# Counting graph edges by keys of destination and a third of the sources instead of by destination alone

## The chip, the cores and the metric

One core of a Trainium2 chip runs the whole kernel. The metric is device time of one execution in microseconds (us), lower is better. Three executions of the kernel before took 1249.06, 1245.67 and 1246.85 us, so the median is 1246.85 us.

## The reference, cut to what matters

The reference is a graph block over N = 1250 nodes with D = 1024 features and E = 20000 edges: a layer norm, a graph attention, a linear attention with Fourier features and an MLP, then a ternary feed-forward. Only the graph attention matters here:

```python
dst = jnp.minimum((1250 * uniform(20000) ** 2.0).astype(int32), 9999)
src, dst = src[argsort(dst)], dst[argsort(dst)]
e = jnp.exp(-leaky_relu(al[src] + ar[dst], 0.1))
rowsum  = segment_sum(e, src, N)
h_prime = segment_sum(e[:, None] * h[dst], src, N) / (rowsum[:, None] + 1e-5)
```

A weight depends only on the pair (src, dst). So the kernel first counts how often each pair occurs, a 1250 by 1250 matrix of small integers, and later multiplies a dense matrix of exponentials by the counts. The edges come sorted by destination, and low destinations are more frequent: the first 125 destinations have 6390 of the 20000 edges, the last 125 have 1048.

## The kernel before, in words

**Data.** The edges are cut into CHUNKS = 160 chunks of T = 125, one edge on each partition. `ends` holds source and destination of each edge as floats. Chunks are handled in groups of HOT = 3.

**A step.** For one chunk and one tile of destinations, VectorE (DVE) writes two matrices of zeros and ones: `hot_s` (125 edges by 1250 sources, line 418) and `hot_d` (125 edges by 125 destinations, line 420). TensorE (PE) multiplies them, as three matmuls of 418, 416 and 416 columns (THIRDS, line 487), and adds up in `p_cnt`, three PSUM banks for a tile, two tiles in turn. HOT slots of the one-hots let VectorE be three steps ahead: it waits on `s_used` (line 416), which line 488 raises, and TensorE waits on `s_hot`.

**The loops.** `tile_onehots(t)` and `count_tile(t)` run for the NT = 10 tiles of destinations. The chunks that touch a tile are known on the chip only, so both engines load the first and last chunk from `span_i` into registers (line 224) and run a hardware loop over groups of three chunks (lines 413 and 482). A chunk that touches two tiles is done in both, and the last group of a tile is filled up, so 60 groups or 180 steps are run (18, 8, 6, 5, 5, 4, 4, 4, 3 and 3 groups). Each tile begins and ends on TensorE with three matmuls of zeros (lines 480, 491).

**Interleaved with it**, by the table AFTER, are ten row tiles of a second layer norm. ScalarE (ACT) takes ten pairs of row sums first (`first_stats`), then scales rows (`normalise`, line 324). TensorE transposes tile i after count tile t if i is in AFTER[t] (line 470, eight transposes). ScalarE applies gain and shift to the eight pieces (`affine`, line 335) and writes the rounded part `x2_hi` (line 340). VectorE subtracts it (`keep_lo(i)`, line 406), which stands in VectorE's program before `tile_onehots(t+2)`. ScalarE also copies each counted tile out of PSUM as 16-bit integers (`keep_counts`, line 319, three instructions), and SyncE (SP) stores it to DRAM in two transfers (`core.move`, lines 82 and 83), from two slots in turn.

**Order at the end of this stage.** All engines meet at a barrier (line 153); then TensorE starts the projections (line 1571), and from there on it is nearly always busy. Much later `attend_over_edges` reads the counts back, a tile of sources at a time (`load_counts`, and one load at the end of the attention stage), for lines 1557 and 709 on VectorE.

Of the kernel before, what the change touches and what calls it, by code (L numbers as in the profile page):

```python
# [6 lines left out]
ALU = mybir.AluOpType  # L7
# [20 lines left out]
HOT = 3  # L28
FF = 512
# [118 lines left out]
def count_and_second_norm(core):  # L148
# [4 lines left out]
    with ExitStack() as ctx:  # L153
# [11 lines left out]
        iota_h = over_lo.put("iota_h", [T, N], FP16)  # L165
        iota_t = over_lo.put("iota_t", [T, NT, 128], FP16)
        tab = over_lo.put("tab", [NT, 3, CHUNKS], F32)
        hit = over_lo.put("hit", [NT, 3, CHUNKS], F32)
        row2 = over_lo.put("row2", [NT, 2, CHUNKS], F32)
        span = over_keys.put("span", [NT, 4], F32)  # L170
        span_i = over_keys.put("span_i", [1, 2, NT], I32)
        hot_s = over_lo.put("hot_s", [T, HOT, N], BF16)
        hot_d = over_keys.put("hot_d", [T, HOT, 128], BF16)
        zeros = over_keys.put("zeros", [T, T], BF16)
        zero_rows = over_keys.put("zero_rows", [T, 418], BF16)
# [6 lines left out]
        p_cnt = ps("p_cnt", [128, 2, 3, 512])  # L182
# [11 lines left out]
        s_iotat = core.sem("tile_iotas_ready")  # L194
# [9 lines left out]
        s_tile = core.sem("tile_counted")  # L204
# [14 lines left out]
        def kept(t):  # L219
            return core.x_in[:, t % 2, 0:N // 2].bitcast(U16)  # L220
# [8 lines left out]
        AFTER = {0: (), 1: (0,), 2: (1, 2), 3: (3, 4), 4: (5,), 5: (6,), 6: (7,), 7: (8,), 8: (9,), 9: ()}  # L229
# [4 lines left out]
        def _(sp):  # L234
# [9 lines left out]
            for t in range(NT):  # L244
                sp.wait_ge(s_kept, t + 1)
                core.move(sp, core.counts_dram[:, :, t, :].rearrange("i p s -> p i s"), kept(t).rearrange("p (i s) -> p i s", i=NT),
                          s_cst[t % 2])

        @block.gpsimd
        def _(pool):  # L250
            pool.memset(core.ident[:], 0.0).then_inc(s_prep, 1)
            pool.iota(iota_h[:], pattern=[[1, N]], base=0, channel_multiplier=0,
                      allow_small_or_imprecise_dtypes=True).then_inc(s_iota, 1)
# [3 lines left out]
            pool.memset(ends[:, CHUNKS:, :], -1.0).then_inc(s_pad, 1)  # L257
            pool.iota(tab[:, 0, :], pattern=[[0, CHUNKS]], base=0, channel_multiplier=T,
                      allow_small_or_imprecise_dtypes=True).then_inc(s_iota, 1)
            pool.iota(tab[:, 1, :], pattern=[[0, CHUNKS]], base=T, channel_multiplier=T,  # L260
                      allow_small_or_imprecise_dtypes=True).then_inc(s_iota, 1)
            pool.iota(tab[:, 2, :], pattern=[[1, CHUNKS]], base=-CHUNKS, channel_multiplier=0,
                      allow_small_or_imprecise_dtypes=True).then_inc(s_iota, 1)
# [38 lines left out]
        def _(act):  # L302
# [11 lines left out]
            def keep_counts(t):  # L314
                act.wait_ge(s_tile, t + 1)
                if t >= 2:
                    act.wait_ge(s_cst[t % 2], MOVED * (t // 2))
                for n, (a, w) in enumerate(THIRDS):
                    last = act.activation(kept(t)[:, a:a + w], p_cnt[0:T, t % 2, n, 0:w], ACT.Copy)
                last.then_inc(s_kept, 1)  # L320
# [23 lines left out]
            keep_counts(0)  # L344
            act.wait_ge(s_rstd, RSTD_STEPS)
            for i in range(NT):
                normalise(i)
                if i == 3:
                    keep_counts(1)
            act.wait_ge(s_gb, 1)  # L350
            for t in range(2, NT):
                for i in AFTER[t - 1]:
                    affine(i)
                keep_counts(t)
                if t == NT - 2:
# [5 lines left out]
        def _(dve):  # L361
# [3 lines left out]
            dve.tensor_reduce(bounds[:, 0, :], edges_f[:, 1], AX.X, ALU.min).then_inc(s_efl, 1)  # L365
            dve.tensor_reduce(bounds[:, 1, :], edges_f[:, 1], AX.X, ALU.max).then_inc(s_efl, 1)
            dve.wait_ge(s_iota, 1)
            dve.tensor_copy(iota_t[:, :, 0:T], iota_h[:].rearrange("p (a b) -> p a b", a=NT)).then_inc(s_iotat, 1)
            dve.wait_ge(s_tr, 1)
            dve.tensor_copy(row2[:].rearrange("p a (g c) -> p a g c", c=2),  # L370
                            p_bound[0:NT, 0:4 * EDGE_ROWS].rearrange("p (a c g) -> p a g c", a=2, c=2)).then_inc(s_ends, 1)
# [6 lines left out]
            dve.wait_ge(s_iota, 4)  # L378
# [20 lines left out]
            dve.tensor_copy(span_i[:], p_span[0:1, 0:2 * NT].rearrange("p (a t) -> p a t", a=2)).then_inc(s_span, 1)  # L399
            dve.wait_ge(s_span, 1)  # L400
            dve.wait_ge(s_iotat, 1)
# [6 lines left out]
            with dve.register("chunks_done") as done, dve.register("first_chunk") as r0, dve.register("past_chunk") as r1:  # L408
                dve.reg_mov(done, 0)

                def tile_onehots(t):
                    first, past = groups_of(dve, t, (r0, r1))
                    with dve.Fori(first, past, HOT) as g:
                        before = dve.snap(done, min_val=0, max_val=NT * (CHUNKS + HOT))
# [9 lines left out]
                tile_onehots(0)  # L424
                dve.wait_ge(s_vt, 1)
                dve.tensor_copy(core.cols[:], p_cols[:, 0:COLUMN_COUNT]).then_inc(s_gb, 1)
                tile_onehots(1)
# [4 lines left out]
                for i in AFTER[NT - 2]:  # L432
                    keep_lo(i)
# [5 lines left out]
        def _(pe):  # L439
# [3 lines left out]
            for a in range(2):  # L443
                for c in range(2):
                    pe.matmul(p_bound[0:NT, (2 * a + c) * EDGE_ROWS:(2 * a + c + 1) * EDGE_ROWS],
                              bounds[:, a, c:c + 1].to_broadcast([EDGE_ROWS, NT]), ident[0:EDGE_ROWS, 0:EDGE_ROWS],
                              start=True, stop=True)
# [2285 lines left out]
```

## Time and profile before

| | |
|---|---|
| median of three executions | 1246.85 us |
| the profiled execution, its own time | 1247.46 us |
| its span, from the first to the last instruction | 1245.7 us |
| TensorE busy | 1187.0 us |
| VectorE busy | 757.5 us |
| ScalarE busy | 704.7 us |
| GpSimd busy | 337.1 us |
| mean granted TensorE clock | 0.984 of full |

Times in the rows are microseconds from the span's start, busy times are sums. A queue's name with a q behind it (DVEq, SPq) is the engine's sequencer, which does register work, branches and waits and hands the other instructions to the engine.

### The profile page before, as it was taken

The page shows a single profiled execution, that of the slowest core. Times are in us where ns is not written, and L with a number is a line of the kernel's source. Part 1 is how long each engine was busy: PE and PEld are TensorE (multiplying, and loading weights), DVE is VectorE, ACT ScalarE, POOL GpSimd, SP SyncE. Part 2 cuts the span into 40 slices and gives each one's busy share as a digit, 9 for nine tenths or more (in the row PEclk, how much of TensorE's full clock was granted, in tenths as well). Part 3 has the DMA queues.
Part 4 walks back from the last instruction along what each step waited for, and adds up shares of the span by engine and source line. Part 5 has one row for each costly group of instructions (what it writes and reads, how often), then busy time and mean ns, then how long its engine had stood idle before and what let it go on. Part 6 is the DMA issues. An engine that isn't in the chain of part 4 may idle for free. (4 is left out here: it accounts for less than half of the span.)

```text
span 1245.7 us, 19482 instructions
## 1 busy us (share of the span) xinstructions
PE 1187.0 (95%) x6857; PEld 1040.2 (84%) x6857; DVE 757.5 (61%) x1248; ACT 704.7 (57%) x1070; POOL 337.1 (27%) x296
## 2 busy tenths in 40 slices
PE   6999998999999999999989999999989998999997
PEld 3555598999999999999978878999978877887884
DVE  7988815656665655665774676777753122556656
ACT  7265617777777777777786333322344332455543
POOL 1500013242414143333122010566635331211100
PEclk9999999999999999999999999999987999999999
DMA  8011140020201202020446566222253332712103
GB/s 221 11 21 29 32 96 1 1 71 0 71 21 50 63 8 71 0 71 0 138 126 215 165 194 203 77 87 87 76 184 99 99 80 71 218 33 66 30 6 99
DMA packets 72195, 99.41 MB, mean 80 GB/s; under 512 B 27242, under 2 KB 52166, under 8 KB 71632
## 3 DMA queue, kind: packets, MB, share of 16 engines
q1 hardware_dynamic: 68684, 86.11, 24.2%
q0 software_dynamic: 3456, 12.58, 3.4%
q8 instruction: 34, 0.56, 0.2%
q14 instruction: 21, 0.16, 0.0%
HBM read 77.04 MB, written 21.63 MB: 79 GB/s over the span
## 5 line engine op out<-in xcount | busy, mean ns | idle before, releaser
L1067 POOL TENSOR_TENSOR cos_sin_lo<-cos_sin,cos_sin_hi 125x1024 fp32r<-125x1024 f32 (+1 forms) x40 | 95.7, 2392 | 245.7 <-ACT cos_sin_hi L1179 245.7
L487 PE MATMUL p_cnt<-hot_s,hot_d 125*125 125x418 bf16 x540 | 113.7, 361 | 1.8 <-DVE hot_d L420 1.8
L418 DVE TENSOR_SCALAR hot_s<-iota_h,ends 125x1250 bf16<-125x1250 f16 x180 | 98.0, 544 | 14.5 <-PE p_cnt L487 12.5
L487 PEld LDWEIGHTS p_cnt<-hot_s,hot_d 125*125 125x125 bf16 x540 | 63.3, 139 | 51.5 <-DVE hot_d L420 40.5
L1571 PE MATMUL rows_in_psum<-x,mix_hi_v 128*128 128x416 f32 (+1 forms) x384 | 105.4, 356 | 0.0
L1571 PE MATMUL rows_in_psum<-x,mix_hi_q 128*128 128x416 f32 (+1 forms) x384 | 104.1, 352 | 0.0
L1571 PE MATMUL rows_in_psum<-x,mix_hi_k 128*128 128x416 f32 (+1 forms) x384 | 103.9, 351 | 0.0
L769 PE MATMUL rows_in_psum<-h_hi,a_lo 125*125 125x342 f32 x300 | 97.0, 323 | 5.9 <-POOL a_lo L611 3.8
L1675 PE MATMUL rows_in_psum<-x,xt_hi 128*125 128x512 f32 x320 | 100.4, 395 | 0.0
L769 PE MATMUL rows_in_psum<-h_hi,a_hi 125*125 125x342 f32 x300 | 96.4, 321 | 0.0
L769 PE MATMUL rows_in_psum<-h_lo,a_hi 125*125 125x342 f32 x300 | 96.4, 321 | 0.0
L1179 ACT ACTIVATE cos_sin_hi<-cos_sin 125x1024 fp32r<-125x1024 f32 (+1 forms) x80 | 83.6, 1045 | 8.2 <-PE rows_in_psum L1653 6.2
L1403 DVE TENSOR_SCALAR whole_turns<-rows_in_psum 125x512 f32<-125x512 f32 (+1 forms) x80 | 54.5, 681 | 39.3 <-PE rows_in_psum L1623 36.5
L2012 PE MATMUL rows_in_psum<-wo_rest,at_hi 128*125 128x512 f32 x280 | 77.4, 399 | 0.0
L1164 ACT ACTIVATE cos_sin<-part_turn 125x512 f32<-125x512 f32 (+1 forms) x80 | 49.8, 623 | 44.2 <-DVE part_turn L1405 43.8
L1571 PEld LDWEIGHTS rows_in_psum<-x,mix_hi_v 128*128 128x128 f32 x384 | 73.1, 191 | 1.0
L1571 PEld LDWEIGHTS rows_in_psum<-x,mix_hi_q 128*128 128x128 f32 x384 | 72.1, 188 | 0.7
L1571 PEld LDWEIGHTS rows_in_psum<-x,mix_hi_k 128*128 128x128 f32 x384 | 72.2, 188 | 0.5
L1571 PE MATMUL rows_in_psum<-x,mix_lo_v 128*128 128x416 f32 (+1 forms) x192 | 69.1, 360 | 3.7 <-PEq L153 3.5
L1675 PEld LDWEIGHTS rows_in_psum<-x,xt_hi 128*125 128x125 f32 x320 | 59.4, 186 | 13.7
L1675 PE MATMUL rows_in_psum<-x,xt_lo 128*125 128x512 f32 x160 | 65.4, 409 | 5.6 <-DVE x L1413 5.5
L1409 DVE TENSOR_TENSOR cos_sin_lo<-cos_sin,cos_sin_hi 128x1000 fp32r<-128x1000 f32 (+1 forms) x40 | 63.2, 1579 | 8.5 <-ACT cos_sin_hi L1179 8.0
(310 smaller groups left out, 3091.3 us busy)
## 6 DMA issues: line engine op xcount, KB each, us to landing
x_in<-in_x_dram SPq DMA_DIRECT2D x30, 448.0 KB
attn_dram<-attn_t SPq DMA_DIRECT2D x8, 625.0 KB, 4.0
at_in<-attn_dram SPq DMA_DIRECT2D x10, 500.0 KB, 4.7
x_rows<-in_x_dram SPq DMA_DIRECT2D x10, 448.0 KB
x_in<-gnn_dram SPq DMA_DIRECT2D x10, 448.0 KB
out_dram<-rows SPq DMA_DIRECT2D x10, 448.0 KB
mix_in_v<-in_L_mix_wv_dram SPq DMA_DIRECT2D x8, 512.0 KB, 6.0
mix_in_k<-in_L_mix_wk_dram SPq DMA_DIRECT2D x8, 512.0 KB, 4.7
```

The lines of the kernel that those rows point to most:

```text
L418: dve.tensor_scalar(hot_s[:, j, :], iota_h[:], ends[:, at, 0:1].rearrange("p a b -> p (a b)"), None, ALU.is_equal)
L487: last = pe.matmul(p_cnt[0:T, t % 2, n, 0:w], hot_d[:, j, 0:T], hot_s[:, j, a:a + w], start=False, stop=False)
L769: last = pe.matmul(p_o[0:T, i % 2, n, 0:H_COLS], stationary(left, i, d), right[:, d, cols], start=(d == 0 and m == 0), stop=(d == NT - 1 a ...
L1067: pool.tensor_tensor(full(cs_lo, k), full(cs, k), f32(full(cs_hi, k)), ALU.subtract).then_inc(s_cslo[0], 1)
L1164: act.activation(step_view(cs, k, 1), rows(part, k), ACT.Sin, scale=TWO_PI)
L1179: act.activation(full(cs_hi, k), full(cs, k), ACT.Copy).then_inc(s_cshi, 1)
L1403: dve.tensor_scalar(flat(whole, k), flat(p_p, k), MAGIC, -MAGIC, ALU.add, ALU.add).then_inc(s_whole, 1)
L1409: dve.tensor_tensor(full(cs_lo, k), full(cs, k), f32(full(cs_hi, k)), ALU.subtract).then_inc(s_cslo[1], 1)
L1571: last = pe.matmul(p_w[:, n, 0:w], left[which][:, k, :], right[:, k, a:a + w], start=(k == 0 and m == 0), stop=(k == K8 - 1 and m == 2))
L1675: last = pe.matmul(p_h(i)[:, n, :], left[i % 2][:, k, :], right[:, k, n * 512:(n + 1) * 512], start=(k == 0 and m == 0), stop=(k == K8 - 1 ...
L2012: last = pe.matmul(p_o[i % 2][0:T, n, :], left[i % 2][:, k, :], right[:, n * 512:(n + 1) * 512], start=(k == 0 and m == 0), stop=(k == K8 ...
```

## The change

The 1250 sources are cut in PARTS_OF_S = 3 parts of S_PART = 417. A key is 3 x destination + part, and there are 3750 keys. The tiles become WINDOWS = 30 windows of 125 keys, and the source one-hots are 420 columns wide instead of 1250. A window's counts are 125 keys by 417 sources, one PSUM bank, four windows in turn (TURNS). Before the tables are made, VectorE splits the edges into keys and sources within a part (five new instructions on 80 by 250 elements). AFTER is spread over the windows, ScalarE copies the first five windows before it normalises, and later normalises tile i+2 just before `affine(i)`.

By the reference's edges the 30 windows take 10, 5, 4, 3, 3, 3, 3 groups, then 22 windows of 2 and the last of 1: 76 groups or 228 steps, against 60 and 180.

```diff
+PARTS_OF_S = 3
+S_PART = -(-N // PARTS_OF_S)
+S_WIDTH = 420
+WINDOWS = NT * PARTS_OF_S
+KEY_SHIFT = N * PARTS_OF_S // 2
+BANK_PIECES = [(0, 420)]
+TURNS = 4 // len(BANK_PIECES)
...
-        iota_h = over_lo.put("iota_h", [T, N], FP16)
-        iota_t = over_lo.put("iota_t", [T, NT, 128], FP16)
+        iota_s = over_lo.put("iota_s", [T, S_WIDTH], FP16)
+        iota_k = over_lo.put("iota_k", [T, WINDOWS, 128], FP16)
...
-        p_cnt = ps("p_cnt", [128, 2, 3, 512])
+        p_cnt = ps("p_cnt", [128, TURNS, len(BANK_PIECES), 512])
...
-        AFTER = {0: (), 1: (0,), 2: (1, 2), 3: (3, 4), 4: (5,), 5: (6,), 6: (7,), 7: (8,), 8: (9,), 9: ()}
+        AFTER = {w: tuple(i for i in range(NT) if w == 6 + i + i // 2) for w in range(WINDOWS)}
+        FIRST_WINDOWS = 5
...
-            for t in range(NT):
+            for t in range(WINDOWS):
                 sp.wait_ge(s_kept, t + 1)
-                core.move(sp, core.counts_dram[:, :, t, :].rearrange("i p s -> p i s"), kept(t).rearrange("p (i s) -> p i s", i=NT),
-                          s_cst[t % 2])
+                core.move(sp, core.counts_of_keys[t * T:(t + 1) * T, :], kept(t), s_cst[t % 2])
...
+            pool.iota(iota_k[:, :, 0:T], pattern=[[T, WINDOWS], [1, T]], base=-KEY_SHIFT, channel_multiplier=0,
                       allow_small_or_imprecise_dtypes=True).then_inc(s_iota, 1)
...
-            keep_counts(0)
+            for t in range(FIRST_WINDOWS):
+                keep_counts(t)
             act.wait_ge(s_rstd, RSTD_STEPS)
-            for i in range(NT):
+            for i in range(2):
                 normalise(i)
-                if i == 3:
-                    keep_counts(1)
             act.wait_ge(s_gb, 1)
-            for t in range(2, NT):
+            for t in range(FIRST_WINDOWS, WINDOWS):
                 for i in AFTER[t - 1]:
+                    if i + 2 < NT:
+                        normalise(i + 2)
                     affine(i)
                 keep_counts(t)
...
+            split_step(dve.tensor_scalar(part_of_s[:], sources, float(S_PART), float(-KEY_SHIFT), ALU.is_ge, ALU.add))
+            for n in range(2, PARTS_OF_S):
+                split_step(dve.scalar_tensor_tensor(part_of_s[:], sources, float(n * S_PART), part_of_s[:], ALU.is_ge, ALU.add))
+            split_step(dve.scalar_tensor_tensor(keys, keys, float(PARTS_OF_S), part_of_s[:], ALU.mult, ALU.add))
+            dve.tensor_reduce(bounds[:, 0, :], keys, AX.X, ALU.min).then_inc(s_efl, 1)
+            dve.tensor_reduce(bounds[:, 1, :], keys, AX.X, ALU.max).then_inc(s_efl, 1)
+            split_step(dve.scalar_tensor_tensor(sources, part_of_s[:], float(-S_PART), sources, ALU.mult, ALU.add))
+            split_step(dve.tensor_scalar(sources, sources, float(-S_PART * KEY_SHIFT), None, ALU.add))
...
-                            dve.tensor_scalar(hot_s[:, j, :], iota_h[:], ends[:, at, 0:1].rearrange("p a b -> p (a b)"), None,
+                            dve.tensor_scalar(hot_s[:, j, :], iota_s[:], ends[:, at, 0:1].rearrange("p a b -> p (a b)"), None,
                                               ALU.is_equal)
-                            dve.tensor_scalar(hot_d[:, j, 0:T], iota_t[:, t, 0:T], ends[:, at, 1:2].rearrange("p a b -> p (a b)"),
+                            dve.tensor_scalar(hot_k[:, j, 0:T], iota_k[:, t, 0:T], ends[:, at, 1:2].rearrange("p a b -> p (a b)"),
                                               None, ALU.is_equal).then_inc(s_hot, 1)
...
-                for t in range(2, NT):
+                window_onehots(1)
+                for t in range(2, WINDOWS):
                     for i in AFTER[t - 2]:
                         keep_lo(i)
-                    tile_onehots(t)
+                    window_onehots(t)
...
-                            for n, (a, w) in enumerate(THIRDS):
-                                last = pe.matmul(p_cnt[0:T, t % 2, n, 0:w], hot_d[:, j, 0:T], hot_s[:, j, a:a + w], start=False, stop=False)
+                            for n, (a, w) in enumerate(BANK_PIECES):
+                                last = pe.matmul(p_cnt[0:T, t % TURNS, n, 0:w], hot_k[:, j, 0:T], hot_s[:, j, a:a + w], start=False, stop=False)
...
-                core.move(sp, counts[:, i % SLOTS], core.counts_dram[i], s_cnt[i % SLOTS])
+                core.move(sp, counts[:, i % SLOTS], core.counts_of_sources[:, :, i * T:(i + 1) * T], s_cnt[i % SLOTS])
...
-        core.counts_dram = nc.dram_tensor("counts_dram", (NT, T, NT, T), U16).ap()
+        core.counts_dram = nc.dram_tensor("counts_dram", (N, PARTS_OF_S * S_PART), U16).ap()
+        core.counts_of_keys = core.counts_dram.rearrange("d (a s) -> (d a) s", a=PARTS_OF_S)
+        core.counts_of_sources = core.counts_dram.rearrange("(t p) s -> p t s", p=T)
```

## Rows read from the trace of the kernel before

**Rows 1.** The page, part 1: busy time of each engine over the span.
```profile
PE 1187.0 (95%) x6857; PEld 1040.2 (84%) x6857; DVE 757.5 (61%) x1248; ACT 704.7 (57%) x1070; POOL 337.1 (27%) x296
```
**Rows 2.** Waits from 13 to 157 us: engine, tile, line, releaser, total, times, longest.
```profile
PEld p_cnt L487 <- DVE hot_d L420: 40.5, 152, 1.4
```
**Rows 3.** Timeline of VectorE: start, duration, engine, line, operation. One step of a tile.
```profile
118.10 0.55 DVE L418 TENSOR_SCALAR hot_s<-iota_h,ends 125x1250 bf16<-125x1250 f16 x1
118.56 0.26 DVE L420 TENSOR_SCALAR hot_d<-iota_t,ends 125x125 bf16<-125x125 f16 x1
118.72 0.54 DVE L418 TENSOR_SCALAR hot_s<-iota_h,ends 125x1250 bf16<-125x1250 f16 x1
```
**Rows 4.** VectorE's sequencer, line 413: all of them, then 119.3 to 121.1 us.
```profile
L413 DVEq FUSED_REGOPS  x60: 58/58/66, 12.9 to 149.7; - x60
...
L413 DVEq FUSED_REGOPS  x2: 58/58/58, 119.6 to 121.0; - x2
```
**Rows 5.** The same line from 65 to 65.9 us, between two tiles.
```profile
L413 DVEq COMPARE_BRANCH  x1: 50/50/50, 65.1 to 65.1; - x1
L413 DVEq FUSED_REGOPS  x1: 58/58/58, 65.8 to 65.8; - x1
```
**Rows 6.** VectorE's sequencer, line 413, at 49 to 50.4 us; PE's timeline before it.
```profile
48.56 0.69 PE L491 MATMUL p_cnt<-zero_rows,zeros 125*125 125x418 bf16 x3
...
L413 DVEq FUSED_REGOPS  x1: 58/58/58, 50.2 to 50.2; - x1
```
**Rows 7.** A `keep_lo` on VectorE's timeline, and line 413 behind it.
```profile
79.00 1.20 DVE L406 TENSOR_TENSOR x<-x_rows,x 128x1000 fp32r<-128x1000 f32 x1 [0.56 <-ACT x L340]
...
L413 DVEq FUSED_REGOPS  x1: 58/58/58, 79.7 to 79.7; - x1
```
**Rows 8.** Timeline of ScalarE, with the PE instruction that releases its copies.
```profile
51.85 4.64 ACT L324 ACTIVATE x_rows<-x_rows,ln_shift,ln_scale 125x1024 f32<-125x1024 f32 x4 [1.22 <-POOL ln_shift L299]
...
93.97 0.69 PE L491 MATMUL p_cnt<-zero_rows,zeros 125*125 125x418 bf16 x3
...
94.70 1.34 ACT L319 ACTIVATE x_in<-p_cnt 125x418 uint16<-125x418 f32 x3 [5.88 <-PE p_cnt L491]
95.91 2.90 ACT L335 ACTIVATE x_rows<-p_t,columns 128x125 f32<-128x125 f32 x8
98.84 1.04 ACT L340 ACTIVATE x<-x_rows 128x1000 fp32r<-128x1000 f32 x1
99.78 2.86 ACT L335 ACTIVATE x_rows<-p_t,columns 128x125 f32<-128x125 f32 x8
```
**Rows 9.** Line 487 at 13.5 to 17.4 us, then 20 to 40 us: minimum, median, maximum ns.
```profile
L487 PE MATMUL p_cnt<-hot_s,hot_d x10: 548/554/608, 13.9 to 17.1; 125*125 125x416 bf16 x6, 125*125 125x418 bf16 x4
...
L487 PE MATMUL p_cnt<-hot_s,hot_d x99: 339/341/391, 19.8 to 39.9; 125*125 125x416 bf16 x66, 125*125 125x418 bf16 x33
```
**Rows 10.** Timeline of the start: VectorE and GpSimd instructions like the added ones.
```profile
1.00 1.18 POOL L252 IOTA iota_h<- 125x1250 f16 x1
...
3.98 0.41 DVE L365 TENSOR_REDUCE bounds<-edges_f 80x2 f32<-80x250 f32 x1
...
10.05 0.23 DVE L393 TENSOR_SCALAR hit<-tab 10x160 f32<-10x160 f32 x1
```
**Rows 11.** Timeline of the stage's end, all engines.
```profile
152.62 0.69 PE L491 MATMUL p_cnt<-zero_rows,zeros 125*125 125x418 bf16 x3
...
154.06 1.31 ACT L319 ACTIVATE x_in<-p_cnt 125x418 uint16<-125x418 f32 x3
...
155.74 0.57 SPq L83 DMA_DIRECT2D counts_dram<-x_in  x1
...
156.84 0.43 PE L1571 MATMUL rows_in_psum<-x,mix_lo_v 128*128 128x418 f32 x1 [3.53 <-PEq L153]
```
**Rows 12.** The first load of the counts and the first instruction that reads it.
```profile
752.87 0.32 SPq L82 DMA_DIRECT2D counts<-counts_dram  x1
...
758.98 0.81 DVE L1557 SCALAR_TENSOR_TENSOR z<-z,counts 125x625 f32<-125x625 f32 x1 [0.80 <-ACT z L1352]
```

More of the change, by code:

```diff
@@ L164, in count_and_second_norm @@
         ends = over_keys.put("ends", [T, CHUNKS + HOT - 1, 2], F32)
-        iota_h = over_lo.put("iota_h", [T, N], FP16)
-        iota_t = over_lo.put("iota_t", [T, NT, 128], FP16)
[L167 to L173, printed above, removed]
+        part_of_s = over_lo.put("part_of_s", [EDGE_ROWS, 2, T], F32)
+        iota_s = over_lo.put("iota_s", [T, S_WIDTH], FP16)
+        iota_k = over_lo.put("iota_k", [T, WINDOWS, 128], FP16)
+        tab = over_lo.put("tab", [WINDOWS, 3, CHUNKS], F32)
+        hit = over_lo.put("hit", [WINDOWS, 3, CHUNKS], F32)
+        row2 = over_lo.put("row2", [WINDOWS, 2, CHUNKS], F32)
+        span = over_keys.put("span", [WINDOWS, 4], F32)
+        span_i = over_keys.put("span_i", [1, 2, WINDOWS], I32)
+        hot_s = over_lo.put("hot_s", [T, HOT, S_WIDTH], BF16)
+        hot_k = over_keys.put("hot_k", [T, HOT, 128], BF16)
         zeros = over_keys.put("zeros", [T, T], BF16)
-        zero_rows = over_keys.put("zero_rows", [T, 418], BF16)
+        zero_rows = over_keys.put("zero_rows", [T, 420], BF16)
         junk = over_lo.put("junk", [T, D], BF16)
@@ L256, in _ @@
                                base=0, pattern=[[-1, 128]], channel_multiplier=1).then_inc(s_ident, 1)
-            pool.memset(ends[:, CHUNKS:, :], -1.0).then_inc(s_pad, 1)
-            pool.iota(tab[:, 0, :], pattern=[[0, CHUNKS]], base=0, channel_multiplier=T,
+            pool.memset(ends[:, CHUNKS:, :], FLT_MAX).then_inc(s_pad, 1)
+            pool.iota(tab[:, 0, :], pattern=[[0, CHUNKS]], base=-KEY_SHIFT, channel_multiplier=T,
                       allow_small_or_imprecise_dtypes=True).then_inc(s_iota, 1)
-            pool.iota(tab[:, 1, :], pattern=[[0, CHUNKS]], base=T, channel_multiplier=T,
+            pool.iota(tab[:, 1, :], pattern=[[0, CHUNKS]], base=T - KEY_SHIFT, channel_multiplier=T,
                       allow_small_or_imprecise_dtypes=True).then_inc(s_iota, 1)
             pool.iota(tab[:, 2, :], pattern=[[1, CHUNKS]], base=-CHUNKS, channel_multiplier=0,
+                      allow_small_or_imprecise_dtypes=True).then_inc(s_iota, 1)
+            pool.iota(iota_s[:], pattern=[[1, S_WIDTH]], base=0, channel_multiplier=0,
+                      allow_small_or_imprecise_dtypes=True).then_inc(s_iota, 1)
+            pool.iota(iota_k[:, :, 0:T], pattern=[[T, WINDOWS], [1, T]], base=-KEY_SHIFT, channel_multiplier=0,
                       allow_small_or_imprecise_dtypes=True).then_inc(s_iota, 1)
@@ L444, in _ @@
                 for c in range(2):
-                    pe.matmul(p_bound[0:NT, (2 * a + c) * EDGE_ROWS:(2 * a + c + 1) * EDGE_ROWS],
-                              bounds[:, a, c:c + 1].to_broadcast([EDGE_ROWS, NT]), ident[0:EDGE_ROWS, 0:EDGE_ROWS],
+                    pe.matmul(p_bound[0:WINDOWS, (2 * a + c) * EDGE_ROWS:(2 * a + c + 1) * EDGE_ROWS],
+                              bounds[:, a, c:c + 1].to_broadcast([EDGE_ROWS, WINDOWS]), ident[0:EDGE_ROWS, 0:EDGE_ROWS],
                               start=True, stop=True)
+            pe.wait_ge(s_split, PARTS_OF_S + 2)
             for a in range(2):
@@ L455, in _ @@
             for a in range(2):
-                last = pe.transpose(p_span[0:1, a * NT:(a + 1) * NT], span[:, a:a + 1], ident[0:NT, 0:NT])
+                last = pe.transpose(p_span[0:1, a * WINDOWS:(a + 1) * WINDOWS], span[:, a:a + 1], ident[0:WINDOWS, 0:WINDOWS])
             last.then_inc(s_spant, 1)
@@ L474, in _, with count_window @@
                 pe.reg_mov(done, 0)
-                def count_tile(t):
-                    if t >= 2:
-                        pe.wait_ge(s_kept, t - 1)
-                    for n, (a, w) in enumerate(THIRDS):
-                        pe.matmul(p_cnt[0:T, t % 2, n, 0:w], zeros[:], zero_rows[:, 0:w], start=True, stop=False)
+                def count_window(t):
+                    if t >= TURNS:
+                        pe.wait_ge(s_kept, t - TURNS + 1)
+                    for n, (a, w) in enumerate(BANK_PIECES):
+                        pe.matmul(p_cnt[0:T, t % TURNS, n, 0:w], zeros[:], zero_rows[:, 0:w], start=True, stop=False)
@@ L488, in count_tile @@
                             last.then_inc(s_used, 1)
                         pe.reg_add(done, done, HOT)
-                    for n, (a, w) in enumerate(THIRDS):
-                        last = pe.matmul(p_cnt[0:T, t % 2, n, 0:w], zeros[:], zero_rows[:, 0:w], start=False, stop=True)
+                    for n, (a, w) in enumerate(BANK_PIECES):
+                        last = pe.matmul(p_cnt[0:T, t % TURNS, n, 0:w], zeros[:], zero_rows[:, 0:w], start=False, stop=True)
                     last.then_inc(s_tile, 1)
-                count_tile(0)
+                count_window(0)
@@ L495, in _ @@
                 pe.wait_ge(core.vectors_loaded, 16 * len(COLUMNS))
                 pe.transpose(p_cols[:, 0:COLUMN_COUNT], core.vectors[:], ident[0:COLUMN_COUNT, 0:COLUMN_COUNT]).then_inc(s_vt, 1)
-                for t in range(1, NT):
-                    count_tile(t)
+                for t in range(1, WINDOWS):
+                    count_window(t)
                     for i in AFTER.get(t, ()):
@@ L1050, in _ @@
                     sp.wait_ge(s_tern, 2 * PIECES)
-                    core.move(sp, core.counts[:, 0], core.counts_dram[0], s_cnt0)
+                    core.move(sp, core.counts[:, 0], core.counts_of_sources[:, :, 0:T], s_cnt0)
                 for n in TERNARY_AT.get(i - 4, ()):
```

46 lines of the change are left out of this document (22 added, 24 removed).

## The prediction

> **What bounds the kernel now.** I read the page's busy times first: TensorE is busy for 1187.0 of the 1245.7 us [rows 1]. Behind the counting stage it hardly ever waits, so what that stage gains or loses moves all the rest by as much. The question is when the first projection matmul starts; it does at 156.84 us [rows 11].
>
> Inside the stage the waits are next: TensorE's weight loads waited 152 times, 40.5 us in all, for the destination one-hot [rows 2]. So in steady counting VectorE is the bound. A step there goes from one `hot_s` to the next, 118.10 to 118.72, that is 0.62 us [rows 3]: 0.46 us for 1250 columns and 0.16 us for 125. Three steps are a group, 1.86 us, and 60 groups are 111.6 us of about 140.
>
> The last view is the one that decides here, VectorE's sequencer. Its loop on line 413 has register work, waits and a branch for every group. Where the engine behind it was busy with a `keep_lo` and the slots were free, the sequencer ran by itself, and went from one pass to the next in 121.0 - 119.6 = 1.40 us [rows 4]. That is hidden under 1.86 us now. It will not be hidden under a shorter group.
>
> **The change, part by part**, in times of the profiled execution, whose own time is 1247.46 us.
>
> *Width of the one-hots.* From 125 to 1250 columns a start-to-start distance grows by 0.30 us [rows 3], so 420 columns take 0.16 + 295 x 0.30 / 1125 = 0.24 us. A step of work is 0.24 + 0.16 = 0.40 us, a group 1.19 us (before rounding). The bounds for 420 columns are the two rows, 0.16 and 0.46 us. The sequencer's 1.40 us a group is longer than 1.19, so I take 1.40 us: 0.47 instead of 0.62 us a step, a quarter less and not the third that the width suggests.
>
> *Number of groups.* They grow from 60 to 76, as each window is rounded up to three chunks and shares chunks with its neighbours. 76 x 1.40 = 106.4 us against 60 x 1.86 = 111.6 us: only 5 us less.
>
> *Borders between windows.* From the last branch of a loop to the next loop it is 65.8 - 65.1 = 0.7 us [rows 5]; the branch stands 1.2 us into its pass, so a border adds (1.2 + 0.7 - 1.4), with the decimals that the rows round off some 0.6 us. The bounds are 0.5 and 0.7. Before, 10 borders were mostly hidden by queued work or `keep_lo`; now there are 30.
>
> *TensorE.* A step falls from three matmuls to one of 420 columns, and a window begins and ends with one matmul of zeros for three. It had slack already, so this frees no time by itself. From the start of the last group's pass to a counted window I reckon 2.06 us: third step after 0.95, one-hots 0.24 + 0.25 [rows 3], then 0.05 to the load, 0.39 for a matmul that has waited (the maximum in [rows 9]), 0.18 for the zeros. The slots suffice: one is free again 1.1 us after its `hot_s` began, under the 1.40 us of a group.
>
> *ScalarE and `keep_lo`, the chain.* Take window a, followed on TensorE by transposes of tile i; a+1, by those of i+1; and a+2, by none. That is the pattern from 6 to 20. When a is counted, ScalarE copies it (0.03 + 0.40, a third of 94.70 to 95.91, [rows 8]), normalises i+2 (1.13, a quarter of 4.64 with overlap), does eight pieces and the rounding of tile i (95.91 to 99.78 = 3.87), copies a+1 (0.40), normalises (1.13), and again 2.93 + 1.04 until `x2_hi` of i+1 is there [rows 8]. Sum 10.9 us. Only then can VectorE do `keep_lo(i+1)`, which stands ahead of window a+3; the next loop pass starts 0.7 us later [rows 7], and window a+3 is counted after 2 x 1.40 + 0.66. That is 15.1 us for three windows, against 3 x (2.8 + 0.6) + 0.2 = 10.4 us of VectorE's own and 11.2 us of ScalarE's. Both stand still part of the time. Before, tiles of three to six groups stood between `affine` and `keep_lo`, and hid more of this.
>
> *The start.* Three of the five new instructions stand ahead of the bounds. 250 columns took 0.41 us in a reduction, 160 took 0.23 us in a one-source instruction [rows 10]; with a wait behind each, 1.35 us. The two others lie beside TensorE's bounds matmuls. The key iota has 3750 columns for the 1250 that took 1.18 us [rows 10], some 3.5 us on GpSimd, ready by 7 us and needed at 14: nothing.
>
> *The sum.* First loop pass 12.9 [rows 4] + 1.35 = 14.3. Window 0, ten groups: 14.0, and 0.66 + 0.95 until the next loop (between those windows `columns` is copied; 49.25 to 50.2 [rows 6]): 29.9. Windows 1 to 6, 21 groups and six borders: 29.4 + 3.5, so 62.8, and window 6 is counted at 62.9. Five times 15.1, less 1.13 twice as tiles 8 and 9 have nothing more to normalise, 73.2: window 21 at 136.1. Windows 22 to 29, 15 groups and seven borders, 25.1, and 0.66: the last is counted at 161.8, where the last tile was at 153.3 [rows 11]. The end gets shorter: before, tile 9's `affine` and three copies lay between that and the barrier, 3.5 us to 156.84; now one copy (0.5), the issue of two stores (0.9) and the barrier (0.5), with `mix_lo` beside them: 2.0. The projections start at 163.8, **7.0 us later**.
>
> Two allowances. Loop passes are not everywhere that short (in one tile of ten the branch came back later), over the 56 groups on the path 1.2 us. And TensorE may run on its lower clock. At the start its matmuls took 554 ns and then 341 ns [rows 9], so a matmul is 0.21 us dearer at 1.2 than at 2.4 GHz; a link of the chain has one counting matmul and one of zeros, and there are seven links: 2.9 us if it stays low throughout, and I take half, 1.5.
>
> The clock is not sure, since a window that is warm uses TensorE for 0.18 of each 0.47 us. The Trainium skill, page "TensorE: Matmul & The Clock Gate", section "Part 1: The HAM clock gate", says that the half clock is the default and that activity releases it. By it the sum would be the whole 2.9 us instead of half if the new loop counts as too little activity, and none if it does not; no row of before shows a loop this sparse.
>
> *What costs nothing.* Stores: 30 pairs of transfers for 10, on a queue that mostly waited; a pair takes some 0.9 us to issue (0.32 in [rows 12] and 0.57 in [rows 11] for one transfer) and a window 3.4 us. They move 834 bytes a row instead of ten pieces of 250. The loads later have the small pieces instead, 1250 a tile. The one with least cover is issued at 752.87 and read at 758.98, after a wait for ScalarE and not for it [rows 12]: 6 us of cover, for a load of the piece size that stores had. If the cover is gone, a few us at most.
>
> Total 7.0 + 1.2 + 1.5 = 9.7 us: 1257.2 for the profiled execution. That lies 0.6 above the median, so **1256.6 us** for the median.
>
> **The rivals.** What this kernel's measurement can tell from no change is about 0.3%, 3.7 us, so the border of slower is 1250.6 and of faster 1243.1.
>
> *B, faster: ScalarE never stands still.* If `keep_lo` of tile i+1 does not hold up window a+3 until TensorE has run dry, the three windows take ScalarE's 11.2 us and not 15.1. Five times 3.9 less is 19.5: 1237.1. It decides as soon as three windows take under 12.4 us. For it: four PSUM banks in turn. Against it: VectorE does things in order, and waited for ScalarE ahead of `keep_lo` already [rows 7]. Chance 0.12.
>
> *C, no change: the sequencer does not bind.* If it keeps ahead of a 0.40 us step, 56 groups are 0.21 us cheaper, 11.8 us in all: 1244.8. Against it stand the passes of 1.40 us [rows 4], with nothing but the sequencer's own work in them. Chance 0.12; for a mixture with B, which also ends within 0.3%, 0.04.
>
> *D, slower by more: the clock stays low,* 2.9 instead of 1.5, and TensorE's transposes also hold up the slots at borders, a further 0.2 us at ten windows or more: 1260. For it, the sparse use; against it, that TensorE was at its full clock through most of the stage. Chance 0.18. A late load of counts or a slower `hot_s` (0.46 us at the upper bound, which would give today's 0.62 us step for 228 steps) would be slower still; 0.04.
>
> **How the numbers follow.** The forecast has 0.50; its own range is 1251.5 to 1260. With D and the late load, slower has 0.68 of the 0.72, as a corner of the forecast's own spread reaches below 1250.6. Faster is B, 0.12, and 0.03 of C's spread below 1243.1. Same has the rest, 0.17. The range from 1243 to 1262 leaves out B and the far end of D.
>
> **What would show it.** In the profile after: `hot_s` at 0.33 us busy and starts 0.47 us apart, in threes, inside a window; idle time of VectorE ahead of line `hot_s` put down to nothing or to "issue"; VectorE's `keep_lo` waiting for ScalarE's `x2_hi` some 2 to 5 us for most of ten tiles; windows 9, 12, 15 and 18 counted 15 us apart; the first projection matmul at 164 to 167 us; and behind it the same distance to the end as now. Starts 0.40 us apart would be C, windows three apart in 11 us B. The forecast is wrong if the projections start before 160 us, or if the time behind their start changes by over 2 us.

## The result, and the profile after

The changed kernel takes **1264.32 us** (median of 4 runs, 1260.66 to 1266.05), the kernel before, run beside it, 1246.53 us: a ratio of 1.0135, interval 1.0106 to 1.0165. It is slower, as forecast, but by 17.8 us where 9.7 were named, and beyond the end of the range. The profiled execution took 1266.05 us, its span is 1264.1 us.

The same view as [rows 1], part 1 of the page of the changed kernel:

```profile
PE 1177.9 (93%) x6545; PEld 1019.7 (81%) x6545; DVE 750.7 (59%) x1348; ACT 706.4 (56%) x1070; POOL 334.1 (26%) x297
```

TensorE, VectorE and GpSimd do less than before and ScalarE 1.7 us more, yet the kernel is 18 us longer. So the time went into standing still, and the place is the counting stage. Its end, on the timeline, answers to [rows 11]:

```profile
170.44 0.38 PE L518 MATMUL p_cnt<-zero_rows,zeros 125*125 125x420 bf16 x1
170.86 0.52 ACT L333 ACTIVATE x_in<-p_cnt 125x417 uint16<-125x417 f32 x1 [1.59 <-PE p_cnt L518]
171.41 0.30 SPq L90 DMA_DIRECT2D counts_dram<-x_in  x1
171.75 1.19 SPq L91 DMA_DIRECT2D counts_dram<-x_in  x1
...
173.47 0.69 PE L1598 MATMUL rows_in_psum<-x,mix_lo_v 128*128 128x418 f32 x1 [2.65 <-PEq L161]
```

The projections start at 173.47 us and not at 156.84: 16.6 of the 18.4 us by which the span grew. The waits from 17 to 172 us (engine, tile, line, releaser, total, times, longest) answer to [rows 2]:

```profile
PEld p_cnt L514 <- DVE hot_k L448: 92.1, 212, 3.0
ACT x_in L333 <- PE p_cnt L518: 68.6, 18, 9.1
...
DVE hot_s L446 <- PE p_cnt L514: 20.3, 30, 1.5
DVE x L434 <- ACT x L354: 16.1, 10, 2.4
```

TensorE waits for VectorE's one-hots 92.1 us instead of 40.5. VectorE itself waits 16.1 us for ScalarE ahead of its ten `keep_lo`, where the same line before (`L406 <- ACT x L340`) had 2.8 us in two waits. ScalarE in turn waits for counted windows. No engine is the bound; a chain that goes round all three is. The 20.3 us in 30 waits are a reading to beware of. 18 of them, 12.7 us, are the borders: 0.66 us for window 3, say, whose pass began at 48.54 in the sequencer, and only then its `hot_s` at 48.76. There TensorE is named because its release came last among those that the profile knows, not because VectorE waited for it. Seven more, 1.9 us, stand in windows 1, 8, 14 and 21, whose passes are slow. But five, 5.7 us, are waits for a slot: in the second pass of windows 7, 10, 13, 16 and 19 VectorE stands still while TensorE is busy with the transposes of the tile before. The first of them, TensorE's row ahead of VectorE's:

```profile
67.94 1.87 PE L497 MATMUL p_t<-ident,x_rows 125*128 125x125 f32 x8
...
70.36 0.33 DVE L446 TENSOR_SCALAR hot_s<-iota_s,ends 125x420 bf16<-125x420 f16 x1 [1.25 <-PE p_cnt L514]
```

These five lie beside ScalarE's longer work: the next `keep_lo` (at 73.70, below) still had to wait 2.05 us for ScalarE, and so did all ten of them, 16.1 us together.

**The step.** The one-hots in the view that groups by line (busy us, mean ns), then line 441 of VectorE's sequencer over the stage and from 147.5 to 150 us, as in [rows 4]:

```profile
L446 DVE TENSOR_SCALAR hot_s<-iota_s,ends 125x420 bf16<-125x420 f16 x228 | 74.2, 326 | 25.5 <-PE p_cnt L514 20.3 <-issue 2.5
L448 DVE TENSOR_SCALAR hot_k<-iota_k,ends 125x125 bf16<-125x125 f16 x228 | 57.8, 254 | 0.0
```

```profile
L441 DVEq FUSED_REGOPS  x76: 58/58/66, 17.5 to 168.5; - x76
...
L441 DVEq FUSED_REGOPS  x2: 58/58/58, 147.9 to 149.3; - x2
```

There are 76 passes, 1.40 us apart inside nearly every window, and `hot_s` takes 0.33 us.

**The chain.** A `keep_lo` on VectorE's timeline answers to [rows 7], and ScalarE's from window 9's copy to window 12's to [rows 8]:

```profile
73.70 1.20 DVE L434 TENSOR_TENSOR x<-x_rows,x 128x1000 fp32r<-128x1000 f32 x1 [2.05 <-ACT x L354]
...
83.88 0.52 ACT L333 ACTIVATE x_in<-p_cnt 125x417 uint16<-125x417 f32 x1 [4.37 <-PE p_cnt L518]
84.29 1.23 ACT L338 ACTIVATE x_rows<-x_rows,ln_shift,ln_scale 125x1024 f32<-125x1024 f32 x1
85.42 2.87 ACT L349 ACTIVATE x_rows<-p_t,columns 128x125 f32<-128x125 f32 x8
88.32 1.04 ACT L354 ACTIVATE x<-x_rows 128x1000 fp32r<-128x1000 f32 x1
...
93.70 1.04 ACT L354 ACTIVATE x<-x_rows 128x1000 fp32r<-128x1000 f32 x1
94.64 0.50 ACT L333 ACTIVATE x_in<-p_cnt 125x417 uint16<-125x417 f32 x1
99.57 0.52 ACT L333 ACTIVATE x_in<-p_cnt 125x417 uint16<-125x417 f32 x1 [4.42 <-PE p_cnt L518]
```

From 83.88 to 99.57 are 15.69 us for three windows; such a stretch is called a link of the chain below. ScalarE works from 83.88 until `x2_hi` of the second tile is there and `keep_lo` starts, at 94.77 (10.9 us, as forecast). It copies one more window, to 95.14, and then stands still 4.42 us, because VectorE begins window 12 only behind a `keep_lo` that had to wait for ScalarE's last instruction. Windows 6, 9, 12, 15 and 18 are counted at 68.15, 83.84, 99.53, 115.22 and 130.91: 15.69 each time.

**The start.** Timeline of GpSimd and VectorE, the kernel before first (one row, not among the rows shown earlier), then after, which answers to [rows 10]:

```profile
3.20 0.74 DVE L363 CAST edges_f<-edges_i 80x500 f32<-80x500 int32 x1 [3.20 <-DMA edges_i<-in_dst_dram]
```

```profile
2.60 3.72 POOL L275 IOTA iota_k<- 125x3750 f16 x1
...
3.19 3.93 DVE L378 CAST edges_f<-edges_i 80x500 f32<-80x500 int32 x1 [3.19 <-DMA edges_i<-in_dst_dram]
...
6.80 0.36 POOL L279 MEMSET minus_half<- 125x10 f32 x1
```

The cast of the edges is the first step of everything that VectorE does in this stage. It takes 3.93 instead of 0.74 us, and the first pass of the loop comes at 17.5 and not at 14.3.

**The clock.** Busy time of each engine and the granted clock (third number from the end, ahead of the DMA share and GB/s) from 17 to 170 us, after, then from 13 to 157 us, before:

```profile
17.00:170.00 153.00, 122.25 (x367) 56.68 (x366) 110.86 (x468) 81.84 (x162) 10.18 (x26) 0.80 0.16 39
```

```profile
13.00:157.00 144.00, 133.26 (x681) 79.94 (x680) 125.97 (x373) 85.12 (x171) 16.27 (x27) 0.99 0.22 49
```

0.80 is a mean of full and half clock, so TensorE had the lower one (1.2 GHz) for 0.40 of 153 us, 61 us; before, hardly ever.

### The profile page after: what moved, and what is told of

Its sections match the earlier page's. It is cut to its first block and busy times, and to the rows that moved or that the text cites. A ratio compares the mean times of both kernels' runs of the same rounds, so it can differ in the third digit from the quotient of the medians.

```text
span 1264.1 us, 19355 instructions
## 1 busy us (share of the span) xinstructions
PE 1177.9 (93%) x6545; PEld 1019.7 (81%) x6545; DVE 750.7 (59%) x1348; ACT 706.4 (56%) x1070; POOL 334.1 (26%) x297
## 5 line engine op out<-in xcount | busy, mean ns | idle before, releaser
L514 PE MATMUL p_cnt<-hot_s,hot_k 125*125 125x420 bf16 x228 | 96.4, 493 | 30.5 <-DVE hot_k L448 29.3
L514 PEld LDWEIGHTS p_cnt<-hot_s,hot_k 125*125 125x125 bf16 x228 | 36.1, 158 | 93.0 <-DVE hot_k L448 92.1
L446 DVE TENSOR_SCALAR hot_s<-iota_s,ends 125x420 bf16<-125x420 f16 x228 | 74.2, 326 | 25.5 <-PE p_cnt L514 20.3
L1598 PE MATMUL rows_in_psum<-x,mix_lo_q 128*128 128x416 f32 (+1 forms) x192 | 67.8, 353 | 0.3 <-DVE xt_lo L1458 0.3
```

The source lines that it names most:

```text
L446: dve.tensor_scalar(hot_s[:, j, :], iota_s[:], ends[:, at, 0:1].rearrange("p a b -> p (a b)"), None, ALU.is_equal)
L514: last = pe.matmul(p_cnt[0:T, t % TURNS, n, 0:w], hot_k[:, j, 0:T], hot_s[:, j, a:a + w], start=False, stop=False)
L1598: last = pe.matmul(p_w[:, n, 0:w], left[which][:, k, :], right[:, k, a:a + w], start=(k == 0 and m == 0), stop=(k == K8 - 1 and m == 2))
```

## Experiments

Theory after the result: the excess has three parts. VectorE's cast lies beside the key table on GpSimd, some 3 us; the chain through ScalarE and `keep_lo` costs four to five us in three windows; the low clock lengthens the chain. The rivals: the cast is slow for another reason; the windows are paced by VectorE alone, not by the chain; the sequencer is not the bound, but the columns; and the clock costs much more, or nothing. The first four kernels are the changed one with one edit each, and ran together, with the kernel before at 1245.53 us.

**a1_no_key_iota.** The table of keys goes; the key one-hot subtracts its window's offset in the same instruction.

```diff
-            pool.iota(iota_k[:, :, 0:T], ...
...
-            dve.wait_ge(s_iota, 5)
+            dve.wait_ge(s_iota, 4)
...
-  dve.tensor_scalar(hot_k[:, j, 0:T], iota_k[:, t, 0:T], ends[...], None, ALU.is_equal)
+  dve.tensor_scalar(hot_k[:, j, 0:T], iota_s[:, 0:T], ends[...],
+                    float(KEY_SHIFT - T * t), ALU.subtract, ALU.is_equal)
```

> The changed kernel without the table of 3750 key numbers on GpSimd; the key one-hot subtracts the key from the first 125 source numbers and compares with a constant of the window. In the changed kernel the cast of the edges took 3.93 us (0.74 before) beside the 3.72 us table. Theory (the two engines got in each other's way): the cast takes 0.7 to 0.8 us again, the first loop pass of VectorE starts at 14.2 to 14.5 us instead of 17.48, and the kernel is 3 to 3.5 us faster than the changed one, near 1261 us. Rival (the cast is slow for the edges' late arrival or for another reason): it stays at 3.9 us and the time stays at 1264. The one-hot keeps 0.25 us; should the second operation cost anything, the passes of 1.40 us still hide it.

Measured: 1257.80 us (1256.85 to 1258.11), ratio 1.0098, interval 1.0081 to 1.0115. Timeline of the start and the first projection:

```profile
3.12 0.10 POOL L276 MEMSET minus_half<- 125x10 f32 x1
...
3.13 0.42 DVE L375 CAST edges_f<-edges_i 80x500 f32<-80x500 int32 x1 [3.13 <-DMA edges_i<-in_dst_dram]
...
169.99 0.69 PE L1595 MATMUL rows_in_psum<-x,mix_lo_v 128*128 128x418 f32 x1 [2.44 <-PEq L161]
```

The cast fell by 3.51 us and the projections start 3.48 us earlier: the table's cost is on the path in full. The medians differ by 6.5 us (5.5 against the kernel before of each batch); the rest arises behind the stage, and isn't put down to the table. From the first projection to the end the traces of all ten kernels take 1085.4 to 1090.7 us, with no edit there; the change has 1090.7, this run 1086.1.

**a2_keep_lo_later.** `keep_lo` moves one window on in VectorE's program, so that window a+3 stands ahead of it.

```diff
-                    for i in AFTER[t - 2]:
+                    for i in AFTER.get(t - 3, ()):
                         keep_lo(i)
```

> The changed kernel with keep_lo(i) one window later in VectorE's program. Theory (from window 6 to 21 the chain through ScalarE's normalise and affine, then keep_lo, then the next window sets the pace, 15.7 us for three windows): the pace falls to ScalarE's own 11.2 to 12.5 us, five such stretches give 16 to 22 us, and the kernel takes 1242 to 1248 us, as fast as the one before. Rival (VectorE's sequencer alone sets the pace in that part too, and keep_lo only fills its gaps): under 4 us faster, 1260 or more.

Measured: 1241.81 us (1240.58 to 1244.11, 10 runs), ratio 0.9970, interval 0.9957 to 0.9983. This one line moves the change from 1.3% slower to a little faster than before (expected were 1242 to 1248). The wait ahead of `keep_lo`, ScalarE's timeline over the same windows, and the first projection:

```profile
DVE x L434 <- ACT x L354: 0.7, 3, 0.2
```

```profile
79.58 0.52 ACT L333 ACTIVATE x_in<-p_cnt 125x417 uint16<-125x417 f32 x1 [0.18 <-PE p_cnt L518]
...
90.35 1.11 ACT L333 ACTIVATE x_in<-p_cnt 125x417 uint16<-125x417 f32 x2
...
154.32 0.69 PE L1598 MATMUL rows_in_psum<-x,mix_lo_v 128*128 128x418 f32 x1 [2.28 <-PEq L161]
```

The waits fall from 16.1 to 0.7 us. Windows 6, 9, 12, 15 and 18 are counted at 68.10, 79.55, 90.90, 102.27 and 113.79, 11.4 us apart and not 15.7, and the projections come 19.2 us earlier. From 79.58 ScalarE goes from one instruction to the next until 90.35 and past it. That is rival B's pace: a mechanism which the order of the program excluded, and which one line brings about.

**a3_narrow_source_onehot.** Half the columns of the source one-hot, and nothing else of the loop. The kernel leaves out the counts of the other half of the sources, so it serves for its time alone.

```diff
+            pool.memset(hot_s[:], 0.0).then_inc(s_zero, 1)
...
+            dve.wait_ge(s_zero, 3)
...
-  dve.tensor_scalar(hot_s[:, j, :], iota_s[:], ends[...], None, ALU.is_equal)
+  dve.tensor_scalar(hot_s[:, j, 0:210], iota_s[:, 0:210], ends[...], None, ALU.is_equal)
```

> The changed kernel, but the source one-hot is only written for the first 210 of 420 columns (the others stay zero, so sources in the upper half of each part are not counted). VectorE's work for a step falls from 0.40 to about 0.35 us. Theory (its sequencer binds with 1.40 us for a pass of three steps): passes stay at 1.40 us, the first window takes as long, and the kernel stays within 2 us of the changed one. Rival (the one-hots' width binds): passes fall by 0.16 us, 76 of them by 12 us in all, and the kernel takes about 1254 us.

Measured: 1261.82 us (1260.23 to 1264.91), ratio 1.0134. `hot_s` is busy 63.4 instead of 74.2 us, the passes stay 1.40 us apart, and the projections start at 173.44 (after 173.47). Its start:

```profile
3.17 5.04 DVE L379 CAST edges_f<-edges_i 80x500 f32<-80x500 int32 x1 [3.17 <-DMA edges_i<-in_dst_dram]
...
6.80 1.14 POOL L279 MEMSET hot_s<- 125x1260 bf16 x1
7.89 0.36 POOL L280 MEMSET minus_half<- 125x10 f32 x1
```

So 10.8 us less work on VectorE bought 1.1 us at most, the lateness of its start. The sequencer is the bound inside a window. The edit also happened to test the cast: one more memset on GpSimd, whose queue ends 1.09 us later, and the cast ends 1.09 us later too.

**a4_more_matmuls.** One more matmul of zeros a step, which keeps TensorE busier and changes no count.

```diff
+  pe.matmul(p_cnt[0:T, t % TURNS, 0, 0:420], zeros[:], zero_rows[:, 0:420], start=False, stop=False)
```

> The changed kernel with a second matmul of 420 columns behind each counting one, zeros by zeros into the same bank, so that the counts stay the same. Theory (a sparse TensorE sits at its lower clock for half of the stage, which costs 0.4 us for each window that someone waits for and a slow start of the projections): the granted clock in the stage rises from 0.78 to 0.95 or more, a window is counted 0.3 us sooner after its last pass, the projections start cold for 3.4 us instead of 6.8, and the kernel is 2 to 5 us faster than the changed one. Rival (the lower clock costs nothing here, or zeros by zeros do not raise it): the clock stays, and the kernel is 0 to 3 us slower for the added work.

Measured: 1263.73 us (1258.96 to 1263.95), ratio 1.0135: no difference from the change, and the expected 2 to 5 us did not come. The same stretch as above:

```profile
17.00:170.00 153.00, 124.54 (x580) 66.18 (x579) 108.85 (x455) 81.45 (x161) 9.95 (x26) 0.96 0.15 39
```

The mean clock rises from 0.80 to 0.96, but the projections start at 176.01, 2.5 us later than after. The mean hides where the low clock is left. The stretches in which windows 9, 12, 15 and 18 are counted:

```profile
80.40:84.10 3.70, 2.76 (x15) 1.58 (x16) 3.03 (x14) 0.33 (x1) 0.00 (x0) 1.00 0.10 28
96.50:99.90 3.40, 3.20 (x9) 2.10 (x10) 2.44 (x11) 0.00 (x0) 0.00 (x0) 0.50 0.05 14
113.60:117.00 3.40, 3.40 (x11) 2.20 (x10) 2.29 (x11) 0.00 (x0) 0.00 (x0) 0.50 0.00 0
130.60:134.10 3.50, 3.50 (x12) 2.31 (x12) 2.55 (x12) 0.00 (x0) 0.00 (x0) 0.51 0.00 0
```

From its first pass to its count window 9 takes 3.73 us here, at the full clock, and 4.07 in the change, at the low one; its link is 15.36 us long and not 15.69. Windows 12, 15 and 18 take 5.07, 5.18 and 5.22 us, at the low clock and with twice the matmuls. So this way of getting the clock back is worth nothing: three of the five links still end at the low clock, and there the added matmuls cost a full us or more each. It is no clean test of what the low clock alone costs. It does show that a link at the full clock is 0.3 us shorter even with the matmuls added.

The second batch asks what the idea is worth when the two faults are gone. The kernel before stood at 1246.35 us.

**b1_both.** Both edits, a1's and a2's.

> The changed kernel with both edits: no table of key numbers, and keep_lo one window later. Alone they gave 6.5 us (3.5 of them at the stage's start) and 22.5 us. Theory (they act at different places, the start and windows 6 to 21): they add, 1236 to 1239 us. Rival (with the start sooner the rest of the stage waits for ScalarE's row statistics and roots, which are not sooner): 1241 to 1242, no better than keep_lo alone.

Measured: 1240.96 us (1238.57 to 1243.95, 7 runs), ratio 0.9948, interval 0.9926 to 0.9970. The projections start at 151.62, 2.7 us ahead of a2's; in the ratio the two can't be told apart from each other. The expected 1236 to 1239 took both gains as additive to the end, and that is not shown: behind the projections' start b1's trace takes 1090.6 us and a2's 1085.8, inside the spread named at a1.

**b2_two_parts.** Both edits, and halves of the sources instead of thirds: 20 windows of 628 columns in two banks, a tile of rows behind each of windows 3 to 12.

```diff
-PARTS_OF_S = 3
+PARTS_OF_S = 2
-S_WIDTH = 420
+S_WIDTH = 628
-BANK_PIECES = [(0, 420)]
+BANK_PIECES = [(0, 314), (314, 314)]
...
-        AFTER = {w: tuple(i for i in range(NT) if w == 6 + i + i // 2) ...
-        FIRST_WINDOWS = 5
+        AFTER = {w: tuple(i for i in range(NT) if w == 3 + i) ...
+        FIRST_WINDOWS = 3
```

> Both edits, and the sources in 2 parts of 625 instead of 3 of 417: 20 windows, 66 groups, one-hots 628 wide (work for a group 0.45 x 3 = 1.35 us), two matmuls a step, two windows in turn, one row tile of the second norm behind each of windows 3 to 12. Theory (VectorE's sequencer: 1.40 us a pass and 0.57 us a border, whatever the width up to some 650 columns): 10 passes and 10 borders fewer, 20 us less counting; with ScalarE's 5.8 us for each of ten windows then as the second bound, the projections start at 122 to 128 us and the kernel takes 1208 to 1216 us. Rival (the width binds: 3.9 columns a ns, 200 steps with 0.05 us more each): it gives back 10 us, 1220 to 1228.

Measured: **1224.51 us** (1223.43 to 1224.83), ratio 0.9813, interval 0.9783 to 0.9842. Faster than both kernels, though 8 us short of what was expected. The time lies in the rival's range, but not for its reason: passes are still 1.40 us apart inside a window that nothing else holds up (128.32 to 129.72 us), so a width of 628 columns doesn't bind either. First projection, then the stretch 60 to 100 us of this kernel, and of the changed one:

```profile
134.59 0.43 PE L1595 MATMUL rows_in_psum<-x,mix_lo_v 128*128 128x418 f32 x1 [2.38 <-PEq L161]
```

```profile
60.00:100.00 40.00, 37.08 (x212) 22.37 (x211) 36.68 (x133) 39.78 (x87) 0.00 (x0) 1.00 0.11 32
```

```profile
60.00:100.00 40.00, 30.22 (x103) 16.25 (x103) 27.12 (x110) 24.50 (x50) 0.00 (x0) 0.75 0.07 20
```

ScalarE is busy 39.78 of 40 us: it has become the bound of the middle, 5.6 us a tile of rows. All three engines and the clock are up from what the change shows. What still costs is the time until then: the first four windows hold 27 of the groups and last until 58.5 us, in which ScalarE has no tile of rows to shift and round yet.

**b3_two_parts_three_turns.** As b2, with three turns of PSUM banks instead of two.

> The same with three windows in turn instead of two (six PSUM banks). Theory (with two, TensorE waits for ScalarE's copy of the window before last only while ScalarE is in an affine, some tenths of a us): within 2 us of the run with two. Rival (the copies gate TensorE): 3 to 8 us faster.

Measured: 1223.93 us (1222.71 to 1224.79), ratio 0.9805, interval 0.9775 to 0.9836; projections at 134.18. The banks are not the bound.

**b4_two_parts_alone.** The halves of b2, but the key table and `keep_lo` where the change has them.

> The changed kernel with 2 parts instead of 3 and one row tile behind each of windows 3 to 12, but with the table of key numbers (2500 of them) and keep_lo where the change has it. Theory: the number of passes and borders is the main cost of the change, and the chain through keep_lo is hidden as windows 5 to 9 are three groups long; 1214 to 1224 us, 4 to 8 us above the run with both edits. Rival (the chain is the main cost here too): 1230 us or more.

Measured: 1231.51 us (1228.42 to 1233.71), ratio 0.9865, interval 0.9830 to 0.9901; projections at 144.30. So without the two edits halves are still faster than before. Two parts instead of three are worth 32.8 us (1264.3 to 1231.5, in different batches), and the two edits a further 7.0, where with three parts they were worth 23: a tile behind each window leaves less for them to mend. The expected 1214 to 1224 was missed by 7.5 us, and the time is the rival's, 1230 or more. The stage is 9.7 us longer than b2's: the first pass comes 2.4 us later, behind a cast of 2.88 us, and windows 4 to 14 come 5.9 us apart on the mean and not 5.1, which makes 7.7 us in ten windows (the rest of the stage is 0.4 us shorter); the profile has 8.2 us of waits ahead of `keep_lo` (b2: none). So the chain is not hidden here either.

## Why the prediction was right in kind and wrong in size

Step by step, at the start of the projections: forecast 163.8 and 2.7 of allowances, 166.5; measured 173.5.

- **Step of work, width, sequencer: right.** `hot_s` 0.33 us, passes of 1.40 us, 76 of them; a3 shows that the columns don't bind. Rival C is out.
- **Borders: right.** Windows of two groups that nothing else holds up are counted 3.37 us apart (144 to 165 us), 2.8 + 0.57.
- **The key iota, "nothing": the step that failed.** The table's cost was put at nothing, and it is 3.2 to 3.5 us on the path. The step named as cover the time until the table is needed at 14 us, and asked only who reads the table. It did not ask what else stands still while GpSimd writes. First pass 17.5, not 14.3: 3.2 us, and a1 gets 3.5 back. The trace of before had a hint of it: its cast of 0.74 us ended at 3.94, with GpSimd's last memset (3.62 + 0.36). With nothing beside it the cast takes 0.42.
- **Windows 0 to 6.** 2.1 us more than forecast, of which 1.2 in window 1: its five passes start at 33.5 to 40.3, 1.70 apart. In the sequencer's own rows the time lies between the branch and the next pass, 0.27 instead of 0.20 us, and between its register instructions. The clock isn't the cause, as window 1 has 1.70 in a4 too, at a clock of 1.00; nor is GpSimd, as the first of these passes takes 1.96 us in a1 as well, from 30.16 us on, where GpSimd is idle until 33.49. It stays open. The allowance for slow passes, 1.2 us over the 56 groups, has just this size, which is luck: it was reckoned from one tile of before in which the branch came back later.
- **The chain: right in kind, 15.7 and not 15.1.** ScalarE 10.9 as forecast, `keep_lo` to the next pass 0.7 as forecast. From the last window's first pass to its count it is 4.07 us where I had 2 x 1.40 + 0.66 = 3.46. With the clock at full it is 3.58 (window 23, 147.93 to 151.51). So 0.1 was sizing and 0.5 the clock; five times, 3.0 us. Another 0.5 us is a slow pass in window 21, and 0.2 is rest. Such a pass of 1.93 us stands in windows 8, 14 and 21, in a2 and a4 as well (in 8 and 14 it is hidden by the wait that follows); the time lies in the sequencer's rows, and why is open. One thing stands beside it in the traces: the DMA queue that the page calls "instruction" (q14) has a transfer of 8 KB that starts within 0.6 us of the end of each, at 76.1, 108.0 and 142.0 us here, at 72.8, 96.8 and 123.0 in a2. So loading of the program's own code may be the cause; no run tests it.
- **The clock, +1.5 of 2.9: too little.** The counting matmuls from 80 to 84 us and from 147.5 to 151 us, at either clock (minimum, median, maximum ns), as in [rows 9]:

```profile
L514 PE MATMUL p_cnt<-hot_s,hot_k x6: 608/610/612, 80.7 to 82.9; 125*125 125x420 bf16 x6
```

```profile
L514 PE MATMUL p_cnt<-hot_s,hot_k x7: 392/392/609, 147.5 to 150.9; 125*125 125x420 bf16 x7
```

  A matmul is 0.22 us dearer at the lower clock, as reckoned from [rows 9]. The last counting matmul and the one of zeros behind it (0.56 us at 83.28, 0.38 at 151.13) stand on the chain: 0.22 and 0.18, 0.40 of the 0.5 us. In five links that makes 2.0 to 2.5 us. The half was wrong: at each of the five windows that ended a link the matmuls were the slow ones. By the Trainium skill, "TensorE: Matmul & The Clock Gate", section "Part 1: The HAM clock gate", the half clock is the default and activity lifts it. The trace agrees, with 0.80 in the sparse loop, and 0.96 once zeros were multiplied there. Behind the stage TensorE began low as well (0.57 from 172 to 180 us), and the span's excess grew from 16.6 to 18.4 us; the forecast had "the same distance behind". That the clock made these 1.8 us is not shown: b1 has 1090.6 us behind the start of its projections, as much as the change, with a clock of 0.80 in its first 8 us.
- **Windows 22 to 29: right,** 25.7 us from window 21's count to the last.
- **The end, 2.0: 2.65 us,** as the issue of the last store took 1.19 us and not 0.57.

The sum: 3.2 + 2.1 + 3.7 + 0 + 0.65 = 9.7 us over 163.8. Allowances had 2.7 of that; 7.0 were missed, and 1.8 more behind the stage. The median was missed by 7.7.

Rival B had its price and point right (11.2 us for three windows, 1237): a2 measures 11.4, and 1241.8. Its condition was not fulfilled, as [rows 7] said. Rival D named the clock, and forecast 1260; the clock did stay low. Its second part, transposes that hold up slots, does show, in five windows and 5.7 us of waits, but they are hidden beside ScalarE and not added to the time. The change itself does less than its width suggests because borders and the sequencer's 1.40 us are paid more often, 30 and 76 times, and because they and the ten `keep_lo` are no longer hidden under 1.86 us of one-hots a group [rows 3].

## What to carry to other kernels

When a stage is made of shorter pieces, look again at each place where an engine does something for another in the middle of its own work: `keep_lo` stood where tiles of three to six groups used to hide it, and moving it on by one window was worth 22 us, 19 of them by the start of the projections. When a table is built on GpSimd, look at what VectorE does in those microseconds, not only at when the table is read. And choose the split by two costs, the width of a one-hot against the 1.40 us of a pass and 0.57 us of a border, which shorter pieces don't lower: with halves instead of thirds and both faults mended, the same idea is 1.9% faster than before.

## What the runs showed of the hardware

- **VectorE's int32 to f32 cast waits for GpSimd.** In five kernels it began at 3.1 to 3.3 us. It ended beside GpSimd's last queued memset, `minus_half`: 3.94 and 3.98 us (before), 7.12 and 7.16 (after), 8.21 and 8.25 (a3), 6.10 and 6.14 (b4); with GpSimd at rest from 3.22 us on it took 0.42 us (a1). The Trainium skill, page "SBUF — State Buffer", section "Who interferes with whom", says that a VectorE cast in a mode with two ports shares a pair of them with GpSimd, and that whoever issues first has the pair for the whole instruction. The runs agree that the cast is fully held up. They add that the larger memsets queued behind the iota went ahead of the waiting cast as well, so the wait is longer than one instruction. The last one seems to have waited in its turn: `minus_half` takes 0.36 us in these four kernels and 0.10 in a1, and 0.42 us back from the cast's end the memset before it was all but over (6.70 us in the trace of after, where `zero_rows` ends at 6.85).
- **A loop on VectorE costs 1.40 us a pass in its sequencer,** with three steps of two instructions with a dynamic address, whether the data instructions need 1.2 us or less. Half the columns change nothing (a3).
- **In a loop with one short matmul each 0.47 us TensorE's granted clock did not stay up:** 61 of 153 us at the lower level, in repeated stretches. The same loop with a matmul of zeros beside each had 0.96.
- **Passes of 1.93 us** in windows 8, 14 and 21, and of 1.60 and more in window 1, at the same place in the change, a1 to a4 and b1, whatever the clock. An 8 KB transfer of the instruction queue starts within 0.6 us of the end of each of the 1.93 us passes. Not explained.
